# Pre-LN linear attention and a spiking MLP on one core: a different order of hand-overs in phase two, a third feature buffer, two banks for the first outputs, and border copies behind elu

## The reference

```python
x = x + attn(layernorm(x))              # x: [4, 2048, 256] float32
x = x + ffn(layernorm(x))

# attn: 16 heads of 64
q, k = elu(x @ Wq) + 1, elu(x @ Wk) + 1
z    = einsum('bhnd,bhd->bhn', q, k.sum(axis=2)) + 1e-6
kv   = einsum('bhnd,bhne->bhde', k, x @ Wv)
out  = einsum('bhnd,bhde->bhne', q, kv) / z
return merge_heads(out) @ Wo + bo
# ffn
h = square(relu(x @ W_fc.T)); y = h @ W_proj.T
# five steps of a leaky threshold unit on y; the mean number of spikes is returned
```

## Time and profile before

| what | value |
|---|---|
| median of 3 runs | 1077.91 us (1075.47 to 1081.84) |
| the profiled execution: its time, its span | 1075.61 us, 1073.8 us |
| PE busy | 1036.8 us, 97% of the span |
| DVE, ACT, POOL busy | 893.2, 723.6, 611.5 us (83%, 67%, 57%) |
| granted TensorE clock, mean | 0.989 |
| chain that ended last, PE's share | 81% |

### The profile page before, as it was taken

The page is one execution under the profiler, slowest core; times in us unless marked ns, Lnnn a source line. Parts: engine busy times, 40 slices in busy tenths (PEclk is TensorE's granted clock), DMA queues, the critical chain, the costliest instruction groups (busy, mean ns, idle before and its releaser), DMA issues.

```text
span 1073.8 us, 18794 instructions
## 1 busy us (share of the span) xinstructions
PE 1036.8 (97%) x6596; PEld 618.2 (58%) x6596; DVE 893.2 (83%) x1871; ACT 723.6 (67%) x1209; POOL 611.5 (57%) x404
## 2 busy tenths in 40 slices
PE   8999999999999988889999999999999999999997
PEld 4444444444444454466666767666676666667666
DVE  7889888798878677898888888888888888888856
ACT  6788677777768644746776766667676666767562
POOL 1443434354445454757867677676766767676632
PEclk9999999999999998989999999999999999999999
DMA  4445543224323424443555444444454444444411
GB/s 138 133 126 137 115 118 94 64 62 117 96 62 93 109 46 84 89 108 84 109 129 102 100 99 99 105 99 111 100 99 99 100 106 96 112 95 89 85 35 35
DMA packets 263086, 104.15 MB, mean 97 GB/s; under 512 B 217296, under 2 KB 260432, under 8 KB 262992
## 3 DMA queue, kind: packets, MB, share of 16 engines
q1 hardware_dynamic: 262992, 102.96, 41.7%
HBM read 33.69 MB, written 16.79 MB: 47 GB/s over the span
## 4 chain that ended last, share of the span: by engine, by line
PE 81%; DVE 8%; ACT 3%; POOL 3%; issue 2%; SPq 2%; DMA 1%; ACTq 0%; DVEq 0%; POOLq 0%
PE proj L522 26%; PE acc L667 14%; PE acc L645 14%; PE acc L550 13%; PE acc L632 12%; DVE spikes L1067 1%; POOL h L1174 1%; DVE feat L912 1%; POOL feat L1146 1%; DVE zsum L991 1%; DMA xT<-xnat 1%; DVE feat L987 1%; ACT h_f L842 1%; DVE xn L902 1%; PE proj L572 1%
## 5 line engine op out<-in xcount | busy, mean ns | idle before, releaser
L1174 POOL TENSOR_TENSOR h<-h_f,h 128x512 f16<-128x512 f32 x128 | 149.3, 1187 | 138.9 <-ACT h L848 138.9
L667 PE MATMUL acc<-wpT,h 128*128 128x256 f16 x1536 | 179.6, 274 | 6.4 <-DVE spikes L1067 6.4
L645 PE MATMUL acc<-xn2T,wfcT 128*128 128x512 f16 x768 | 178.6, 383 | 5.0 <-DMA xn2T<-xnat 5.0
L632 PE MATMUL acc<-m_all,qT 128*128 128x256 f16 x1488 | 175.1, 275 | 6.6 <-DVE x L1079 6.6
L522 PE MATMUL proj<-xn2T,xT 128*128 128x512 f16 x768 | 177.8, 382 | 3.7 <-DMA xT<-xnat 3.5
L550 PE MATMUL acc<-feat,xnat 128*128 128x512 f16 x768 | 176.2, 379 | 0.2 <-DVE feat L957 0.2
L1154 POOL TENSOR_TENSOR feat<-feat 128x1024 f16<-128x1024 f32 x60 | 130.8, 2181 | 79.8 <-ACT feat L800 79.8
L632 PEld LDWEIGHTS acc<-m_all,qT 128*128 128x128 f16 x1488 | 146.5, 99 | 38.4 <-issue 8.4
L522 PE MATMUL proj<-wq,xT 128*128 128x512 f16 x720 | 165.2, 379 | 1.7 <-DVE feat L912 1.1
L667 PEld LDWEIGHTS acc<-wpT,h 128*128 128x128 f16 x1536 | 150.7, 98 | 27.6 <-DVE spikes L1067 8.5
L800 ACT ACTIVATE feat<-feat 128x1024 f16<-128x1024 f32 x60 | 63.4, 1057 | 123.8 <-POOL feat L1146 123.8
(11 more groups left out here) (93 smaller groups left out, 1494.8 us busy)
## 6 DMA issues: line engine op xcount, KB each, us to landing
x_t<-in_L_attn_x_dram SPq DMA_DIRECT2D x128, 128.0 KB, 2.3
xT_spill<-xT SPq DMA_DIRECT2D x64, 128.0 KB, 2.0
out_dram<-out_t SPq DMA_DIRECT2D x64, 128.0 KB, 2.1
xT<-xT_spill SPq DMA_DIRECT2D x60, 128.0 KB, 2.3
ks_all<-ks_rows SPq DMA_DIRECT2D x4, 512.0 KB, 4.2
m_all<-in_L_attn_Wk_dram SPq DMA_DIRECT2D x4, 256.0 KB, 4.6
xT<-xnat SPq DMA_TRANSPOSE x64, 2.4
m_all<-in_L_ffn_W_fc_dram SPq DMA_DIRECT2D x4, 256.0 KB, 3.5
```

What stands on the lines that cost most here:

```text
L632: mm = pe.matmul(acc[:, 0, 0:D], qT_at(n)[:, left * PAIRS + j, :], m_at(n // BT, right, j), start=(i == 1), stop=(i == PAIRS * len(PRODUCTS)))
L645: mm = pe.matmul(acc[:, 2 + f % 2, :], wfcT[:, left, f * C2 + c2, :], xn2T[:, c % 2, right * C2 + c2, :], start=(i == 1), stop=(i == C2 * ...
L667: mm = pe.matmul(y_at(n), h[:, c % 2, left, f, u * P:(u + 1) * P], wpT[:, right, f::FB, :], start=(i == 1), stop=(i == FB * len(PRODUCTS)))
L1174: pool.tensor_tensor(h[:, c % 2, LO, f, :], h_f[:, k % 4, :], h[:, c % 2, HI, f, :], ALU.subtract).then_inc(h_lo, 1)
```

## The change

Phase one: `copy_g` moves in both loops behind the iteration's `k_exp_tile` (ACT) or `k_elu_tile` (DVE). Feature buffers: `feat` holds three tiles. q tiles rotate over three, and `q_exp_tile(n)` waits for `q_lo` of tile n - 3. Phase two, hand-overs: ACT does q_exp ahead of the f1 blocks, q_hi for tile t - 1, and xn_hi last; POOL does q_lo of t - 2, then the normalisation of q of t - 1, the bias of t, and h_lo last; DVE takes `xn_lo` out of the end of a step to the start of the next one; SP turns q of t - 2. First steps: o of tiles 0 to 3 is made in steps 3 and 4, in turn in banks 0 and 1, and kv of the last batch goes to bank 2; the layer norms of these tiles stand ahead of the q steps; q_tile(7) is in step 5, and f1 and f2 of the first chunk each begin a step earlier. The number and size of the instructions on the compute engines stay as they are.

```diff
-        feat = sb("feat", [P, 2, HD], F32)
+        feat = sb("feat", [P, 3, HD], F32)
...
-            return feat[:, n % 2, :]
+            return feat[:, (n - EARLY) % 3, :]
...
+        def o_bank(n):
+            return acc[:, n % 2 if n < 4 else 0, 0:D]
         def o_step(n):
-            return {0: 3, 1: 4, 2: 5, 3: 5}.get(n, n + 3)
+            return 3 + n // 2 if n < 4 else n + 3
+        def lo_step(n):
+            return o_step(n) + (1 if n < 4 else 2)
         def f1_step(n):
-            return n + 7 if n < 4 else n + 9
+            return n + 6 if n < 4 else n + 9
         def f2_step(n):
-            return n + 11 if n < 4 else n + 13
+            return n + 10 if n < 4 else n + 13
... SP
-                for n in at(o_step, t - 2):
+                for n in at(lo_step, t):
                     turn_xn2(n)
...
-                    turn_q(t - 1)
+                    turn_q(t - 2)
... PE
-                wait_past(pe, x2_done, n)
+                wait_past(pe, x2_done, n - 1 if n < 4 else n)
...
+                if t == 5:
+                    m_job(B - 1, 0)
+                    q_tile(EARLY + 3)
+                if t > 6 and live(t + 1):
                     q_tile(t + 1)
+                if t == 6:
+                    pe.wait_ge(chain_free, through("m", B - 1, 0))
+                    m_job(B - 1, 1)
+                    pe.wait_ge(chain_free, len(JOBS))
...
+                for n in at(f1_step, t):
+                    f1_quarter(n)
+                for n in at(o_step, t):
+                    o_tile(n)
                 if t == 4:
                     ks_job(B - 1)
                     kv_job(B - 1)
... ACT
-                wait_past(act, q_lo, n - 1)
+                wait_past(act, q_lo, n - 1 if n < EARLY else n - 2)
...
+                if t < 7:
+                    for n in at(o_step, t - 1):
+                        xn_hi_b(n)
+                if t in (5, 6):
+                    m_hi_job(B - 1, t - 5)
+                if t > EARLY and live(t + 1):
+                    q_exp_tile(t + 1)
                 blocks = [2 * n + i for n in at(f1_step, t) for i in range(2)]
... relu, square, h_hi
-                if t >= EARLY and live(t):
-                    q_hi_tile(t)
+                if t > EARLY and live(t - 1):
+                    q_hi_tile(t - 1)
+                if t >= 7:
+                    for n in at(o_step, t - 1):
+                        xn_hi_b(n)
... DVE, phase one (ACT alike, behind k_exp_tile)
-                if 1 < n < TILES and n % BT == 1:
-                    copy_g(n // BT - 1)
...
                 if live(n) and n - 1 not in GUESTS:
                     k_elu_tile(n)
+                if 1 < n < TILES and n % BT == 1:
+                    copy_g(n // BT - 1)
... DVE, phase two
+                if t < 7:
+                    for n in normal:
+                        newton(ln2, n)
+                        normalise(ln2, x2_at(n), n)
+                    for n in fresh:
+                        residual(n)
+                        stats_b(n)
+                    for n in normal:
+                        xn_lo(ln2, n)
+                    if t == 4:
+                        take_ks(B - 1)
+                        take_kv(B - 1)
+                    if t in (5, 6):
+                        m_lo_job(B - 1, t - 5)
+                else:
+                    for n in at(lo_step, t):
+                        xn_lo(ln2, n)
... the q and spike steps; behind them, for t >= 7: newton, normalise, residual, stats_b
... POOL
-            normalise_q(EARLY)
-            for n in range(2):
+            for n in range(4):
                 bias_x(n)
             for t in STEPS:
-                if t - 1 >= EARLY and live(t - 1):
-                    q_lo_tile(t - 1)
+                if t - 2 >= EARLY and live(t - 2):
+                    q_lo_tile(t - 2)
+                if t > EARLY and live(t - 1):
+                    normalise_q(t - 1)
+                if t >= EARLY and live(t):
+                    bias_x(t)
                 for n in at(f1_step, t):
                     h_lo_block(2 * n)
                     h_lo_block(2 * n + 1)
-                if live(t - 1):
-                    bias_x(t - 1)
-                if t > EARLY and live(t):
-                    normalise_q(t)
```

More of the change, by code:

```diff
@@ L631, in o_tile @@
                         i += 1
-                        mm = pe.matmul(acc[:, 0, 0:D], qT_at(n)[:, left * PAIRS + j, :], m_at(n // BT, right, j),
+                        mm = pe.matmul(o_bank(n), qT_at(n)[:, left * PAIRS + j, :], m_at(n // BT, right, j),
                                        start=(i == 1), stop=(i == PAIRS * len(PRODUCTS)))
@@ L676, in _ @@
                     pe.wait_ge(m_hi, PAIRS)
[L677 removed]
+                if t == 5:
+                    m_job(B - 1, 0)
+                    q_tile(EARLY + 3)
+                if t > 6 and live(t + 1):
                     q_tile(t + 1)
[L679 to L684 removed]
+                if t == 6:
+                    pe.wait_ge(chain_free, through("m", B - 1, 0))
+                    m_job(B - 1, 1)
+                    pe.wait_ge(chain_free, len(JOBS))
+                    pe.wait_ge(m_hi, B * PAIRS)
+                    for i in range(4):
+                        pe.wait_ge(w_turned[i], 64)
+                for n in at(f1_step, t):
+                    f1_quarter(n)
+                for n in at(o_step, t):
+                    o_tile(n)
                 if t == 4:
@@ L688, in _ @@
                     kv_job(B - 1)
-                if t == 5:
-                    m_job(B - 1, 0)
-                if t == 6:
-                    pe.wait_ge(chain_free, through("m", B - 1, 0))
-                    m_job(B - 1, 1)
-                if len(tiles) > 1:
-                    o_tile(tiles[1])
-                if t == f1_step(0):
-                    pe.wait_ge(chain_free, len(JOBS))
-                    pe.wait_ge(m_hi, B * PAIRS)
-                    for i in range(4):
-                        pe.wait_ge(w_turned[i], 64)
-                    f1_quarter(0)
                 for n in at(f2_step, t):
@@ L1102, in _ @@
                     write_out(n)
-                normal, fresh = at(o_step, t - 1), at(o_step, t)
-                for n in normal:
-                    newton(ln2, n)
-                    normalise(ln2, x2_at(n), n)
-                for n in fresh[:1]:
-                    residual(n)
-                for n in normal:
-                    xn_lo(ln2, n)
-                for n in fresh[:1]:
-                    stats_b(n)
-                if t == 4:
-                    take_ks(B - 1)
-                    take_kv(B - 1)
-                for n in fresh[1:]:
-                    residual(n)
-                    stats_b(n)
-                if t in (5, 6):
-                    m_lo_job(B - 1, t - 5)
+                if t >= 7:
+                    for n in normal:
+                        newton(ln2, n)
+                        normalise(ln2, x2_at(n), n)
+                    for n in fresh:
+                        residual(n)
+                        stats_b(n)
         @block.gpsimd
```

27 lines of the change are left out of this document (6 added, 21 removed).

## The result

**The change gains 7.3 us where 16.4 were forecast.** The median after is 1072.34 us (1070.77 to 1076.47, 15 runs), that of before beside it 1079.65 (1075.47 to 1081.84, 15 runs). The ratio is 0.994, 95% interval 0.9928 to 0.9953, a gain of 5 to 8 us. The forecast was 1061.5 with a range of 1055 to 1072, so the time lies just above the range, and the gain is under half of the forecast. The profiled execution of after took 1073.8 us (span 1072.0). That is only 1.8 under the one of before, because the one of before, at 1075.6, is at the low end of its runs. The two traces are therefore compared stretch by stretch, with their repeats, and not by their spans.

What follows compares the result with a forecast made beforehand. PE was taken as the bound, full steps costing their matmuls' 10.42 us. Borders 4.8, first steps 10.4 and behind step 62 1.2 sum to 16.4, taking 1075.6 to 1059.2; median 2.3 higher, 1061.5, range 1055 to 1072.

Steps and rivals of the forecast that it cites:

- The borders: Phase one, borders 17, 33 and 49: moving the copies behind exp and elu gains 4.8 us, between 2 and 5.
- the tight fit: Border 17, no guest as cover: the copies just meet g's requests; gain 1.4 us if they fit, 0 if not.
- Rival (4): The borders give nothing because the DVE copy keeps g waiting: 1066 us, chance 0.08.
- The ring: Phase two's first steps: POOL and ACT wait for each other in a circle of 9.27 us per turn.
- Its start: Phase two's first steps: q_lo(4) ends at 410.3 us, so the circle of POOL and ACT waits starts at 410.35.
- Behind step 62: After step 62: PE's wait for the spikes shrinks because the spike chain starts about 1.5 us earlier; gain 1.2 us.
- rival (2): First steps: late loads for bias(4) and bias(5) and a delayed M eat the gain there: 1072 us, chance 0.10.
- the walk from f1(0) to full step 18: Phase two's first steps: step 18 begins at 511.0 instead of 522.2; 12.6 us gained, 10.4 after clock loss.
- rival (1): Full steps: POOL locks out DVE's xn_lo at the step's head, making f2 wait for spikes: 1083 us, chance 0.13.
- The clock: First steps: a lower clock behind the 4.4 us wait ahead of f1(0) costs 2.2 us.
- rival (3): First steps: the clock falls several times, at o(7) and later waits too, 2 to 2.5 us each: 1066, chance 0.12.
- a wait on bias in full steps: Full steps: a sign that would upset the prediction if seen; no size given.

Runs made afterwards that it cites:

- borders_only: The kernel before with only the border copies moved behind elu: 1073.31 us, ratio 0.995 to before.
- xnlo_behind: The changed kernel with DVE's xn_lo behind the q and spike steps from step 7 on, and SP's layer-norm transpose behind turn_q: 1069.4 us, ratio 0.9906 to before.
- phase_two_only: The changed kernel with its border copies put back ahead of elu: 1076.88 us, ratio 0.9967 to before.
- m_first: The changed kernel with the low part of M's second half ahead of tile 5's q steps on DVE in step 6: 1070.32 us, ratio 0.9919 to before.
- ring_early: m_first plus the q work of tile 4 (normalisation, high and low part) ahead of the bias instructions and step 3: 1069.17 us, ratio 0.9911 to before.
- spikes_ahead: ring_xnlo with each DVE spike step ahead of the q step in steps 8 to 10: 1069.4 us, ratio 0.9896 to before.
- xnlo_mid: The changed kernel with xn_lo behind the first q and spike step from step 7, SP's layer-norm transpose ahead of turn_q: 1091.44 us, ratio 1.0117 to before.
- after again: The changed kernel run unchanged once more for a second profile: 1072.91 us, ratio 0.9943 to before.
- ring_xnlo: The changed kernel with the edits of ring_early and xnlo_behind together: 1068.23 us, ratio 0.9882 to before.

## Why the prediction was wrong

**What held.** What bounds the kernel: full steps cost 10.42 before and after, and only PE's losses moved. The borders: 4.8 forecast, some 3.7 in the traces and 5 (3 to 8) in timed runs; g at border 17 did not wait, so the tight fit was right, but the wait on a transposed tile behind it stayed, and the one at about 351 grew from 0.53 to 1.31. Rival (4) is refuted by borders_only. The ring: 9.27 forecast, 9.44 measured. Its start: q_lo(4) ended 37.7 us behind the start of `q_tile(4)` (407.99 - 370.25), forecast 37.8 (410.3 - 372.46). Behind step 62: 1.2 forecast, 0.9 measured. The median, 1072.34, is the time that rival (2) gave, but that is luck: its mechanism, late loads ahead of bias(4) and bias(5), did not occur. The two began at 401.07 and 405.19, with loads forecast for 403 and 407.5 on a scale that begins 2.2 later.

**The step that failed is the walk from f1(0) to full step 18**, the term of 12.6 - 2.2 = 10.4. Counted from the start of `q_tile(4)`, with the clock charge of 2.2 put in, the walk falls short of the trace of after in these places:

| from, to | forecast | after | short by |
|---|---|---|---|
| q_tile(4) to f2(0) | 75.3 (445.6 + 2.2 - 372.46) | 77.6 | 2.2 |
| f2(0) to f2(1) | 9.9 | 13.0 | 3.1 |
| f2(1) to f2(2) | 8.7 | 10.6 | 1.8 |
| f2(2) to f2(4), with steps 14 to 16 | 44.2 | 44.6 | 0.4 |
| f2(4) to f2(5) | 10.4 | 13.2 | 2.8 |
| f2(5) to f2(6) | 10.4 | 11.8 | 1.3 |

That is 11.6 us, all of the missing gain of this stretch (10.4 forecast, -1.3 in this pair of traces). Two statements of the prediction are behind it.

First, "f1 of a step asks only for the relu of the step before, 2.8 us into the ring, so PE may run up to 6.5 us ahead of it". That is true of f1 and false of f2. f2 waits for the spikes, the spikes stand in DVE's list behind xn_lo, and xn_lo waits for the last work of ACT's turn. I had entered this edit as a gain only, in the tail ("no ACT result is awaited in the middle"), and did not walk it through the first steps, where the ring is late. xnlo_behind shows it: the wait at f2(5) falls from 2.66 to none, that at f2(1) from 4.39 to 2.15, though that second number proves little, as phase_two_only shows.

Second, the price of DVE's work in these steps was made of undisturbed durations: "four q steps of tile 5, which also hold 1.22 us and more". The prediction had the exclusion of DVE and POOL before it (it says that the long products end when a POOL instruction ends; in the trace of before, the one of 3.42 us ends 1.1 us behind one, which is about its own 1.21: it began its work there), and put it into rival (1), for full steps, as something that happens there or not at all. It happens in the first steps, where DVE has no slack. The Trainium skill (SBUF — State Buffer, Who interferes with whom) says that DVE and GpSimd share one pair of ports, that whoever takes it first shuts the other out for a whole instruction, and names beside operations with two SBUF inputs also tensor_scalar among those that can take it. By that rule the trace agrees, with a `zeps` of 2.00 to 2.11 us for 0.16. I used only the half of the rule on two inputs. m_first and ring_early bring f1(0) forward by 2 to 4 us of waiting and the total by 2 to 3, since the following waits take up the rest. This second part is argued from durations for the waits behind f1(0).

**How much is shown.** The best traces of the first steps (187.49 in spikes_ahead, 188.52 in xnlo_behind) are 2.6 to 3.6 us under the mean of 191.1 that the change's phase two takes, of 11.6 that the walk fell short. So the experiments show causes for a quarter to a third of what is missing; for the rest, readings of durations are all there is.

**Rival (1)** did not occur in after, and xnlo_mid shows that its mechanism is real: xnlo_mid, with a stretched xn_lo among the spike steps, takes 19 us more than after (1091.44 - 1072.34). In its trace some 12 of them lie in full steps, since every second one takes 10.98 to 11.08 instead of 10.42, 3 in the first steps and most of the rest behind step 62. The rival had the instruction at the head of the step, where it does not decide.

**The clock.** I charged 2.2 for one fall. In after it fell at f1(0), f2(1) and f2(5): 1.3, 1.4 and 1.3 us over the full-clock durations (4.08, 4.21, 4.12 against 2.75, 2.78, 2.79). That is rival (3)'s mechanism, for f2(1) and f2(5) at waits that the walk did not have. At o(7), which rival (3) named, the clock held in after and fell in after again.

**What stays open:** what would remain of the waits at o(7) and f2(2) if POOL did nothing while DVE does zeps, xn_lo and the normalisation of xn. Whether ring_xnlo is better than xnlo_behind or ring_early: three medians within 1.2 us do not tell. And what the bias costs. In before POOL added it for tile t - 1, and from 410 us on it never waited for the load of x. The change moved it to tile t, ahead of h_lo. SP issues that load in the same step, behind the transpose of the layer norm, which waits for xn_lo, and in steps 11 to 14 of after POOL waits 2.33 to 5.71 us for it:

```profile
469.81 0.73 POOL L1182 TENSOR_TENSOR x_t<-x_t,bo_all 128x256 f32<-128x256 f32 x1 [5.71 <-DMA x_t<-in_L_attn_x_dram]
```

The prediction named a wait on bias in full steps as a sign against it. There it came five times in after, 0.85 us at most, and PE never idled for it. In none of the experiments with the new hand-overs was the bias put back, so its part in the late f2 is untested.

## What to carry to other kernels

When an operation is moved to the head of an engine's list, ask for whom everything behind it now waits: a wait that costs nothing in steps with slack ties the whole list to its slowest partner in steps without. Follow a moved step on every queue it touches, the issuing one too; the same edit gained 3 us or lost 5 to 6 by the order of two transposes on SP. And when two engines exclude each other, price the busy one's instructions as stretched wherever it has no slack, even those with 16 numbers a row.

## What the runs showed of the hardware

- A DVE instruction on 128 x 16 numbers can last as long as a POOL instruction on 128 x 1024: zeps 0.16 us alone, 2.00 when it fell on POOL's q_lo of 2.12.
- The same matmul group behind the same wait of 2.99 or 3.00 us ran at full clock in one execution (2.78 us) and not in two others (4.40 and 4.25). At o(7) of the kernel after, a wait of 3.86 us kept the full clock (2.79) and one of 2.84, in another execution of the same program, did not (4.33). The prediction took 3.00 (kept) and 3.09 (lost) for a boundary; these rows show none.
- A shorter wait is not all gained. Where m_first shortened f1(0)'s wait by 1.97 us, f1 itself took 1.19 longer at a lower clock; in ring_early, behind a wait of only 2.76, it took 5.30 us as against 2.75 at full clock.
